# The first block's y multiplied in fp32 straight from x as loaded, in a Trainium2 kernel of a per-sample projection and a Strassen-like matrix product

## The reference

```
W = weights[condition]                        # [64, 64, 64], one of 16 matrices for each batch
y = einsum('bct,bcd->bdt', x, W)              # x [64, 64, 1024]
...
logits = y_flat @ gate_w.T + expert_bias      # y seen as [4096, 1024]
one_hot = one_hot(argmax(logits))             # 4 experts
base_out = y_flat @ W_up.T                    # W_up [1024, 1024]
z = einsum('nh,erh->ner', y_flat, lora_A)     # rank 8
delta = einsum('ner,ehr->neh', z, lora_B), of the chosen expert
out = x + base_out + delta
```

## Time and profile before

| what | value |
|---|---|
| median of 3 runs | 439.74 us (439.55 to 440.65) |
| the profiled execution | 439.54 us |
| its span in the trace | 437.7 us |
| mean granted TensorE clock | 0.999 of 2.4 GHz |
| PE busy | 431.4 us, 99% of the span |
| DVE busy | 371.2 us, 85% |
| ACT busy | 199.9 us, 46% |
| POOL busy | 121.1 us, 28% |

### The profile page before, as it was taken

The page is one execution under the profiler, slowest core; times in us unless marked ns, Lnnn a source line. Parts: engine busy times, 40 slices in busy tenths (PEclk is TensorE's granted clock), DMA queues, the critical chain, the costliest instruction groups (busy, mean ns, idle before and its releaser), DMA issues.

```text
span 437.7 us, 8630 instructions
## 1 busy us (share of the span) xinstructions
PE 431.4 (99%) x2970; PEld 402.3 (92%) x2971; DVE 371.2 (85%) x659; ACT 199.9 (46%) x310; POOL 121.1 (28%) x95
## 2 busy tenths in 40 slices
PE   8899999999999999999999999999999999999997
PEld 8789999998999999999999999999999999999996
DVE  3999889898897979899797979979798988979773
ACT  5896436362443636254263625335363624436310
POOL 3992032040504013050502205050311405040130
PEclk9999999999999999999999999999999999999999
DMA  9900031140403113050313214041311405031202
GB/s 212 405 34 1 2 127 66 49 146 25 168 24 120 48 65 127 24 168 24 120 48 95 97 48 144 24 145 47 105 63 48 144 24 168 24 120 48 74 24 96
DMA packets 17373, 38.71 MB, mean 88 GB/s; under 512 B 3854, under 2 KB 4110, under 8 KB 17362
## 3 DMA queue, kind: packets, MB, share of 16 engines
q1 hardware_dynamic: 12130, 23.34, 14.8%
q10 hardware_dynamic: 5072, 14.94, 11.5%
q0 software_dynamic: 160, 0.28, 0.3%
HBM read 21.78 MB, written 16.78 MB: 88 GB/s over the span
## 4 chain that ended last, share of the span: by engine, by line
PE 96%; DVE 2%; POOL 1%; ACT 1%; issue 0%; POOLq 0%
PE bank_x L612 22%; PE bank_y L612 22%; PE bank_c L612 19%; PE y_ps L548 12%; PE bank_b L612 10%; PE bank_x L670 2%; PE bank_y L618 1%; PE bank_x L618 1%; PE bank_c L618 1%; PE bank_b L618 1%; PE bank_y L649 1%; PE y_ps L573 1%; PE bank_y L595 1%; DVE w_s L817 1%; PE bank_c L627 0%
## 5 line engine op out<-in xcount | busy, mean ns | idle before, releaser
L314 POOL TENSOR_TENSOR s_sum<-a 128x512 f32<-128x512 f32 x16 | 20.8, 1300 | 287.9 <-DVE a L789 287.9
L784 DVE TENSOR_TENSOR x_hl<-x_sb,x_hl 64x1024 fp32r<-64x1024 f32 x64 | 78.2, 1221 | 8.8 <-ACT x_hl L377 6.9
L377 ACT ACTIVATE x_hl<-x_sb 64x1024 fp32r<-64x1024 f32 x64 | 67.5, 1055 | 38.4 <-DMA out_dram<-x_sb 34.8
L381 ACT ACTIVATE y_small<-y_ps 128x512 f32<-128x512 f32 x62 | 37.0, 597 | 67.2 <-PE y_ps L548 67.2
L548 PE MATMUL y_ps<-cond_hl,x_hl 128*128 x496 | 64.4, 273 | 1.2 <-issue 1.0
L548 PEld LDWEIGHTS y_ps<-cond_hl,x_hl 128*128 128x128 f32 x496 | 60.6, 191 | 3.2 <-issue 1.2
L789 DVE TENSOR_TENSOR a<-y_ps,y_small 128x512 f32<-128x512 f32 x62 | 42.6, 687 | 16.7 <-ACT y_small L381 16.7
L612 PE MATMUL bank_x<-w_a,hl_a 128*128 128x256 f32 (+1 forms) x408 | 54.3, 289 | 0.0
L612 PEld LDWEIGHTS bank_x<-w_a,hl_a 128*128 128x128 f32 x408 | 52.7, 189 | 0.5
L612 PE MATMUL bank_y<-w_s,hl_s 128*128 128x292 f32 (+1 forms) x384 | 51.5, 290 | 0.3 <-DVE hl_s L794 0.3
L612 PE MATMUL bank_x<-w_s,hl_s 128*128 128x292 f32 (+1 forms) x384 | 51.5, 290 | 0.0
(11 more groups left out here) (131 smaller groups left out, 564.1 us busy)
## 6 DMA issues: line engine op xcount, KB each, us to landing
out_dram<-x_sb SPq DMA_DIRECT2D x63, 256.0 KB, 2.0
x_sb<-in_x_dram ACTq DMA_DIRECT2D x28, 512.0 KB, 3.8
w_raw<-in_L_ffn_W_up_dram SPq DMA_DIRECT2D x8, 512.0 KB, 11.9
x_sb<-in_x_dram SPq DMA_DIRECT2D x4, 512.0 KB, 12.1
cond_sb<-in_L_cond_weights_dram ACTq DMA_DIRECT2D x1, 256.0 KB, 5.4
cond_sb<-in_L_cond_weights_dram SPq DMA_DIRECT2D x1, 256.0 KB, 6.5
out_dram<-x_sb SPq DMA_DIRECT2D x2, 128.0 KB, 1.9
router_sb<-in_L_ffn_lora_A_dram POOLq DMA_DIRECT2D x1, 128.0 KB, 7.5
```

Of the source, the lines that this page charges most:

```text
L314: pool.tensor_tensor(s1_sum[:, :], a21[:, :], a22[:, :], ALU.add).then_inc(s1_added, 1)
L377: act.activation(x_hl[rows, t, b, :], x_sb[rows, 2 * par + t, :], ACT.Copy).then_inc(x_high, 1)
L381: act.activation(to[:, :].rearrange("q (g d) -> q g d", d=D), halves_of(bank)[:, :, 1, :], ACT.Copy).then_inc(y_small_out, 1)
L784: dve.tensor_tensor(x_hl[other, t, b, :], x_sb[rows, 2 * par + t, :], x_hl[rows, t, b, :].bitcast(fp32), ALU.subtract).then_inc(x_low, 1)
```

## The change

Block 0's y is made by a new function, `make_first_y`, from x_sb and cond_sb as they were loaded, both fp32, on 64 partitions and with 64 columns to a matmul. There are as many matmuls as before, 32, and each makes its full result, so that ACT alone moves it to a11, a12, a21 and a22 (`move_first_y`); the four ACT and four DVE instructions that split x of block 0 and DVE's four sums fall away. The matmuls read both operands on the lower 64 partitions. Batches 1 and 3 lie on the upper 64 in x_sb, so they are loaded a second time, to the lower ones, in x_first, which lies over x_hl. The splits of the condition matrices stay, for block 1 on, and are no longer waited for by block 0's y.

```diff
+        early = ExitStack()
+        x_first = early.enter_context(nc.sbuf_tensor("x_first", [C, 2, 2, T], fp32))
+        early.close()
...
-        FIRST_Y = [(y_ps, y_small), (bank_x, s1_sum), (bank_y, s2_sum), (y_ps, y_small)]
+        FIRST_Y = [y_ps[:, 0, :], y_ps[:, 1, :], bank_x[:, 0, :], bank_x[:, 1, :]]
+
+        def first_rows(t):
+            return x_first[:, t, 1, :]
...
             sp.dma_start(x_sb[:, 0, :], x_pairs[0]).then_inc(x_loaded[0], 16)
-            sp.dma_start(cond_sb[C:2 * C, :, :], cond_rows).then_inc(cond_loaded, 16)
             sp.dma_start(index_sb[:, :], cond_index.rearrange("(a n) -> a n", a=1)).then_inc(index_loaded, 16)
+            sp.dma_start(first_rows(0), x[1]).then_inc(first_loaded[0], 16)
             sp.dma_start(x_sb[:, 1, :], x_pairs[1]).then_inc(x_loaded[1], 16)
+            sp.dma_start(first_rows(1), x[3]).then_inc(first_loaded[1], 16)
+            sp.dma_start(cond_sb[C:2 * C, :, :], cond_rows).then_inc(cond_loaded[1], 16)
...
+            def move_first_y(n, to):
+                act.wait_ge(y_done, n + 1)
+                act.activation(to[:, :], FIRST_Y[n], ACT.Copy).then_inc(y_summed, 1)
...
-            split_x(0, 0, 0, False)
-            act.wait_ge(cond_loaded, 32)
-            act.activation(cond_hl[:, :, 0, :], cond_sb[:, :, :], ACT.Copy).then_inc(cond_high, 1)
             act.wait_ge(ident_done, 1)
...
-            split_x(0, 0, 1, False)
-            move_small_y(0, 0, 0, *FIRST_Y[0])
+            move_first_y(0, a11)
+            move_first_y(1, a12)
+            for h in range(2):
+                act.wait_ge(cond_loaded[h], 16)
+            act.activation(cond_hl[:, :, 0, :], cond_sb[:, :, :], ACT.Copy).then_inc(cond_high, 1)
+            move_first_y(2, a21)
+            move_first_y(3, a22)
...
+            def make_first_y(t, h, index):
+                pe.wait_ge(x_loaded[t], 16)
+                if h == 0:
+                    pe.wait_ge(first_loaded[t], 16)
+                for k in range(KH):
+                    for b in range(2):
+                        at, cols = k * P + b * D, slice((h * KH + k) * P, (h * KH + k + 1) * P)
+                        rows = first_rows(t)[:, cols] if b else x_sb[0:C, t, cols]
+                        mm = pe.matmul(FIRST_Y[2 * t + h][:, at:at + D], rows, cond_sb[0:C, index[b], :],
+                                       start=True, stop=True)
+                mm.then_inc(y_done, 1)
...
-            pe.wait_ge(cond_low, 1)
-            make_y(0, 0, 0, index[0], FIRST_Y[0][0])
+            pe.wait_ge(cond_loaded[0], 16)
+            make_first_y(0, 0, index[0])
+            make_first_y(0, 1, index[0])
+            make_first_y(1, 0, index[1])
+            make_first_y(1, 1, index[1])
             turn_weights("a11", 0)
```

More of the change, by code:

```diff
@@ L136, in adaln_ffn_kernel @@
         bias_zero = sem("bias_zero")
-        cond_loaded = sem("cond_loaded")
+        cond_loaded = [sem(f"cond_loaded{h}") for h in range(2)]
+        first_loaded = [sem(f"first_loaded{t}") for t in range(2)]
         index_loaded = sem("index_loaded")
@@ L363, in _ @@
         def _(act):
[L364 removed]
+            act.dma_start(cond_sb[0:C, :, :], cond_rows).then_inc(cond_loaded[0], 16)
             def load_x(q, par, t):
@@ L454, in _ @@
             split_turned("s4", 0)
-            move_small_y(0, 0, 1, *FIRST_Y[1])
             split_turned("a11", 1)
             split_turned("a12", 1)
-            move_small_y(0, 1, 0, *FIRST_Y[2])
             split_turned("s2", 0)
             split_turned("s1", 0)
+            split_turned("a11", 2)
+            round_a11(0, False)
             round_a12(0, False)
-            split_turned("a11", 2)
-            move_small_y(0, 1, 1, *FIRST_Y[3])
-            round_a11(0, False)
             split_turned("s1", 1)
@@ L495, in _ @@
             split_turned("lora", 1)
+            act.wait_ge(cond_low, 1)
             round_a22(0, False)
@@ L537, in load_index, with make_y @@
                         for b in range(2)]
-            def make_y(q, t, h, index, bank=None):
+            def make_y(q, t, h, index):
                 if h == 0:
[L541 to L544, removed]
+                    pe.wait_ge(x_low, 4 * q + 2 * t - 2)
+                pe.wait_ge(y_summed, 4 * q + 2 * t + h)
                 for k in range(h * KH, (h + 1) * KH):
@@ L547, in make_y @@
                         at = (k % 2) * 2 * P + b * P
-                        mm = pe.matmul(bank[:, k % KH // 2, at:at + P], x_hl[:, t, b, k * P:(k + 1) * P],
+                        mm = pe.matmul(y_ps[:, k % KH // 2, at:at + P], x_hl[:, t, b, k * P:(k + 1) * P],
                                        cond_hl[:, index[b], :, :], start=True, stop=True)
+                mm.then_inc(y_done, 1)
[9 more added lines that the diff above has]
+                                       start=True, stop=True)
                 mm.then_inc(y_done, 1)
@@ L586, in turn_weights @@
                         pe.wait_ge(t4_added, OH)
+                        pe.wait_ge(cond_low, 1)
                         src = w_raw[:, c, HALF:T]
@@ L901, in after_delta22 @@
                 add_bank(bank_b, par, 1, 1).then_inc(c22_out, 1)
-            for b in range(2):
-                split_x(0, 0, 0, b)
             dve.wait_ge(cond_high, 1)
@@ L907, in _ @@
                               ALU.subtract).then_inc(cond_low, 1)
-            for b in range(2):
-                split_x(0, 0, 1, b)
             split_turned("a11", 0)
@@ L912, in _ @@
             split_turned("s4", 0)
-            sum_y(a11, 0, 0, 0, *FIRST_Y[0])
             split_turned("a11", 1)
             split_turned("a12", 1)
-            sum_y(a12, 0, 0, 1, *FIRST_Y[1])
             split_turned("s2", 0)
-            sum_y(a21, 0, 1, 0, *FIRST_Y[2])
             split_turned("s1", 0)
             split_turned("a11", 2)
-            sum_y(a22, 0, 1, 1, *FIRST_Y[3])
             low_operand("a11", a11, 0)
```

24 lines of the change are left out of this document (9 added, 15 removed).

## The result

The changed kernel takes 450.76 us (median of 4 runs, 449.11 to 452.47) beside 439.78 us of the kernel before: a ratio of 1.0246, 95% interval [1.0203, 1.029]. It is 11 us slower, 2 us above the forecast range. The profiled execution took 452.47 us, its span 450.7 us (437.7 before).

The account below looks back on a forecast made before the run. Two equally long chains, PE with ACT and DVE, and POOL alone, were taken to set when "a22" starts, PE being solid behind it. y's delay of POOL, +4.8 us with all else hidden or nothing, gave 444.5 us, range 440.9 to 448.8.

Parts of the forecast that it names:

- y's start: PE after its warm-up: block 0's y still starts at 12.14, since PE did not wait for splits before; worth nothing.
- y's length: Block 0's 32 fp32 matmuls on PE: each costs two of today's, 0.21 us, together 6.8 us.
- y's place: All of y ahead of the first turned piece: POOL's t1(0) starts at 19.47 instead of 14.68, +4.8 us.
- The other chain: PE, ACT and DVE turning pieces: DVE's first moves +3.3 us, first product ends near 34.2, inside the 4.8 us.
- DVE's sums, splits, waits on cond_low: Block 0's start: 2.4 us of DVE sums and eight splits of x go, cond_low's split runs later; no gain or loss.
- Transfers: 0.5 MB more on the queue before W_up: last piece 0.9 to 1.5 us late, hidden by POOL's 4.8 us.
- From "a22" to the end: Rest of the program after the "a22" transposes start: lasts as long as before, 407 us.
- four-loads rival: Each fp32 y matmul has four loads, 0.31 us; y 10.0 us, 447.7 us; between two and four loads, chance 0.22.
- full price: Each of an fp32 matmul's four products costs a full y matmul: y 13.6 us, +11.6, 451.3 us; above 448.5, chance 0.06.
- "faster" rival: y within 2.0 us keeps POOL's start and POOL's subtractions don't hold "a22": 437.3 us; chance 0.03.
- cheap-y rival: An fp32 matmul costs one pass, or one of today's: y 2.5 or 3.4 us, 440.6 to 441.2; chance 0.17.

Follow-up runs that it names:

- half rows without fp32: Kernel before the change plus 128 unused fp32r matmuls of 64 partitions and 64 columns ahead of block 0's first y; 467.61 us, one run.
- full-row kernel: Changed kernel with its 32 fp32 y matmuls on 128 partitions instead of 64, condition matrices back in their queue place; 445.81 us, ratio 1.0135.
- block-diagonal version: Kernel before, block 0's y from 16 fp32 matmuls with two batches' condition matrices on a zeroed 128x128 diagonal; 438.84 us; with last t4 on DVE 440.82.
- a kernel with 64-row y (446.07): Changed kernel with y pieces between turned pieces, condition matrices back in their queue place, last t4 on DVE; 450.48 us over six runs, fastest 446.07.

## Why the prediction was wrong

The path was right, the size was not: 11.0 us of loss for 4.8. By its own steps:

- *y's start:* 12.36 for 12.14. Right.
- *y's length:* **this step failed.** 6.8 us were forecast and 12.15 measured. Its count of the work was right: two matmul rows and two loads for each fp32 matmul, 0.222 us at full clock, and 0.23 with full rows. What it took for granted was the clock of the rows it priced with. At half clock the same instruction took 0.426 us. Of the 5.35 us too little, 0.3 to 0.6 us are the unit price and the rest the clock. The clock fell with matmuls on 64 of the 128 partitions: full rows with the same fp32 matmuls kept it, half rows without fp32 lost it. It did not fall equally far in every run.
- *y's place:* t1(0) waits for the "a11", 0 transposes, as forecast, but starts at 25.71 instead of 19.47. The 6.24 us between are y's start 0.22, its length 5.35, four transposes at half clock 0.58 and a slower hand-over 0.09. Behind it POOL lost 0.46 us more, most of it (0.44) in waiting for the "a11", 2 transposes. These ran at full clock, but late: ahead of them PE had waited 1.0 us for DVE. With the forecast 4.8 us this makes 11.5 us, which is what t4 and a22 show.
- *The other chain:* right that it stays inside POOL's shift: the first product ended at 41.46, t4 at 42.09. Wrong that DVE's pieces would be no wait of PE's: PE waited for them twice behind 27 us, 1.0 us each. A third wait that the profile puts down to DVE, 0.7 us ahead of a22, ended with POOL's t4; this is the gap that was forecast, at 1.2 us.
- *DVE's sums, splits, waits on cond_low:* forecast to be worth nothing. No run takes them by themselves; with POOL's chain ending last, nothing in the traces speaks against it.
- *Transfers:* mis-sized. By themselves they cost 3.6 us, not 0.9 to 1.5, by the first piece of W_up and by PE's idle time, not by the last piece. In the changed kernel they are hidden up to a22: y ended at 24.51, and in the kernel with "a11", 0 first, whose queue is the same, the first piece had landed at 15.4. In the full-row kernel too (y ended at 19.2).
- *From "a22" to the end:* 408.5 us instead of 407. Of this 0.75 us are lost in block 1, where a store takes 4.36 us to land (70.81 to 75.17), which also happened without the change. Some 0.6 us more come in small steps over the other blocks, in the kernels with the change's y and its x_first (not in the one with the extra loads alone); the cause stays open. So does what makes that store late.

The four-loads rival (447.7, or 451.3 at the full price) came nearest in time by luck, not by mechanism: the number of loads was two, and the price of its rows was that of the full clock. The "faster" rival's condition, y short enough to keep POOL's start, is what the block-diagonal version met; a22 followed POOL's t4 there all the same (29.82 and 29.96). The cheap-y rival's floor was too low: at full clock a small matmul with its load took 0.11 us with 64 columns as with 128. The prediction's chances, added up by its own terms, give slower 0.91, same 0.06 and faster 0.03, where 0.90, 0.07 and 0.03 are stated.

The rule taken from the page "FP8 and Floating Point Precision" of the Trainium skill, section "TensorE Precision Notes", four passes for true fp32, left open how often weights load. The rows show two loads and two matmuls to an instruction; whether the four passes lie in them the trace does not tell.

## What to carry to other kernels

A price read from a row holds at the clock of that row. Before using it for new work, ask what share of the array the new instruction fills: matmuls on 64 of 128 partitions were followed by a clock at half, 0.426 us for 0.222, and the transposes behind them took twice the time too, on an engine that looked 100% busy. If half the rows are free, fill them, be it with zeros: the block-diagonal form halves the matmuls and keeps the clock. When an edit adds transfers to a queue, follow the first transfer behind them, not only the last, and ask what stands idle until it lands.

## What the runs showed of the hardware

- The granted clock fell to half with PE busy for 100% of the time, 2.0 us behind the first matmul of 64 partitions (4.4 us where no gap came before it), and stayed there for 13.7 us, over the full-row transposes too. In one run of a kernel with 64-row y (446.07) the mean clock was 1.000. Of the changed kernel's runs the fastest (449.11) has a mean clock of 0.989, the profiled one 0.985: some 10 us at half clock instead of 13.5. That is 1.8 us of the 3.4 between the two; the runs at 0.985 lie 2.4 us apart by themselves.
- Idle time went before a fall too: with the extra loads alone PE was idle for 2.5 us behind its warm-up and first y piece, and the clock was at half for 3.4 us of full-row work.
- An fp32 matmul at full clock takes 0.22 us with 64 partitions and columns, 0.23 with 128 partitions and 64 columns, 0.25 with 128 and 128.
- POOL's four copies of lora_b took 1.42 us in the changed kernel and 3.02 before, where DVE's splits of x ran beside them. Of the 13 traces six have no DVE work beside these copies, 1.42 us each; four have the splits beside them, 3.0 to 3.4 us; the other three, with DVE at work beside a part of them, 2.2 to 2.4. What makes them slower no run isolates.
